# A decoder layer on one core: shared values tiles in cross attention, and self attention's buffers cleared earlier

## The reference

```
x = layernorm(x + self_attention(x))          # causal, scores relu(q k) * table(w, v), softmax, @ Wo + bo
x = layernorm(x + cross_attention(x, ctx))
x = layernorm(x + down(silu(gate(x)) * up(x)))   # int32 weights / 127, hidden size 1536

def cross_attention(query, ctx):
    q = query @ Wq.T + bq;  k = ctx @ Wk.T + bk;  v = ctx @ Wv.T + bv      # ctx: (32, 722, 512)
    probs = softmax(q k / sqrt(32))                                        # per head, over the 722 keys
    return (probs @ v) @ Wo.T + bo
```

## Time and profile before

| | |
|---|---|
| median of 3 runs | 2468.52 us (2468.2 to 2473.67) |
| the profiled execution | 2468.12 us |
| its span | 2466.3 us |
| PE busy | 2378.6 us (96%) |
| DVE, ACT, POOL busy | 1540.8 (62%), 1323.6 (54%), 1320.3 (54%) |
| chain that ended last | PE 74%, the D_ps_p units (L68) alone 42% |
| self attention | 0 to about 360 us |
| cross attention | 539 to about 1960 us |

### The profile page before, as it was taken

The page is one execution under the profiler, slowest core; times in us unless marked ns, Lnnn a source line. Parts: engine busy times, 40 slices in busy tenths (PEclk is TensorE's granted clock), DMA queues, the critical chain, the costliest instruction groups (busy, mean ns, idle before and its releaser), DMA issues.

```text
span 2466.3 us, 58741 instructions
## 1 busy us (share of the span) xinstructions
PE 2378.6 (96%) x21728; PEld 2050.7 (83%) x21728; DVE 1540.8 (62%) x2621; ACT 1323.6 (54%) x3287; POOL 1320.3 (54%) x1130
## 2 busy tenths in 40 slices
PE   7999968999999999999999999999999899999999
PEld 6887847888888888888888888888888698998998
DVE  7666677846666766666766667666676725335342
ACT  4777762116666666666666666666666651221311
POOL 4677563326565665656666566665655533333332
PEclk9999989999999999999999999999999999999999
DMA  6777676625767666666666676666767841101010
GB/s 196 198 224 203 191 201 251 242 104 147 191 187 195 188 183 187 189 191 190 185 189 187 190 192 186 185 188 188 196 187 191 233 149 64 39 26 61 2 39 23
DMA packets 271021, 404.21 MB, mean 164 GB/s; under 512 B 126364, under 2 KB 146332, under 8 KB 270748
## 3 DMA queue, kind: packets, MB, share of 16 engines
q1 hardware_dynamic: 246172, 350.25, 49.0%
q10 hardware_dynamic: 24576, 50.36, 8.1%
HBM read 134.11 MB, written 52.43 MB: 76 GB/s over the span
## 4 chain that ended last, share of the span: by engine, by line
PE 74%; DVE 1%; issue 1%; POOL 1%; ACT 0%; SPq 0%; DMA 0%; ACTq 0%; POOLq 0%; DVEq 0%
PE D_ps_p L68 42%; PE D_ps_s L1800 7%; PE D_ps_p L1826 6%; PE E_ps_g L68 5%; PE E_ps_u L68 5%; PE E_ps_d L68 5%; PE E_ps_y L68 3%; DVE D_columns L1611 0%; PE E_ps_t L1852 0%; SPq L1252 0%; DMA E_w_int<-in_w_gate 0%; ACT D_e L1476 0%; POOL D_e L1360 0%; DVE D_turned L1625 0%; POOL E_acts_low L1409 0%
## 5 line engine op out<-in xcount | busy, mean ns | idle before, releaser
L1360 POOL TENSOR_SCALAR D_e<-D_e,D_columns 128x722 f32<-128x722 f32 x256 | 538.9, 2105 | 528.2 <-DVE D_columns L1617 528.2
L1476 ACT ACTIVATE D_e<-D_ps_s,D_columns 128x723 f32<-128x723 f32 x512 | 438.2, 862 | 408.7 <-DVE D_columns L1611 358.2
L1611 DVE TENSOR_REDUCE D_columns<-D_ps_s 128x1 f32<-128x723 f32 x512 | 439.7, 900 | 303.1 <-PE D_ps_s L1800 302.9
L1625 DVE STREAM_TRANSPOSE D_turned<-D_e 128x768 f32<-128x768 f32 x512 | 496.4, 973 | 5.1 <-DMA D_pT<-D_turned 4.0
L68 PE MATMUL D_ps_p<-D_ctx_high,cross_wk_high 128*128 128x362 f32 (+1 forms) x1024 | 350.0, 342 | 1.5 <-DVEq L1637 1.5
L68 PE MATMUL D_ps_p<-D_ctx_low,cross_wk_high 128*128 128x362 f32 (+1 forms) x1024 | 336.6, 329 | 0.0
L68 PE MATMUL D_ps_p<-D_ctx_high,cross_wk_low 128*128 128x362 f32 (+1 forms) x1024 | 335.0, 327 | 0.0
L68 PE MATMUL D_ps_p<-cross_wv_high,D_ctx_high 128*128 128x512 f32 (+1 forms) x768 | 303.9, 396 | 0.0
L68 PE MATMUL D_ps_p<-cross_wv_high,D_ctx_low 128*128 128x512 f32 (+1 forms) x768 | 303.3, 395 | 0.0
L68 PE MATMUL D_ps_p<-cross_wv_low,D_ctx_high 128*128 128x512 f32 (+1 forms) x768 | 301.8, 393 | 0.0
L1483 ACT ACTIVATE D_e<-D_e,D_columns 128x722 f32<-128x722 f32 x256 | 230.9, 902 | 6.1 <-DVE D_columns L1617 6.1
(11 more groups left out here) (217 smaller groups left out, 5095.9 us busy)
## 6 DMA issues: line engine op xcount, KB each, us to landing
D_pT<-D_turned SPq DMA_DIRECT2D x1536, 96.0 KB, 2.7
D_pT<-D_turned ACTq DMA_DIRECT2D x512, 96.0 KB, 2.8
D_craw<-in_ctxT SPq DMA_DIRECT2D x124, 361.0 KB, 4.0
self_q<-A_q_out SPq DMA_DIRECT2D x10, 640.0 KB, 4.1
self_k<-A_k_out SPq DMA_DIRECT2D x10, 640.0 KB, 3.8
self_v<-A_v_out SPq DMA_DIRECT2D x25, 256.0 KB, 3.6
A_q<-self_q SPq DMA_DIRECT2D x32, 200.0 KB, 3.6
A_k<-self_k SPq DMA_DIRECT2D x32, 200.0 KB, 4.1
```

Of the source, the lines that this page charges most:

```text
L1360: pool.tensor_scalar(head, head, inv[:, 2 * (s % 2):2 * (s % 2) + 1], None, ALU.mult)\
L1476: act.activation(e[n // 2 % 2][:, n % 2, 0:PARTS * PART].rearrange("p (a c) -> p a c", a=PARTS), parts_of(n), ACT.Exp, bias=neg_max[:, n % ...
L1611: dve.tensor_reduce(neg_max[:, n % 4:n % 4 + 1], parts_of(n), AX.XY, ALU.max, negate=True)\
L1625: dve.transpose(turned[quad % 2][:, :, 2 * (s % 2) + h, :].rearrange("p j (t r) -> p t j r", r=32), e[s % 2][:, h, :].rearrange("p (t j r) ...
```

## The change

**Values.** Of the 32 batches the first 28 (`SHARED`) go in groups of four. The sixth values unit of a group's first three batches gets a stationary tile of its own, `tails`: columns 0 to 81 are the batch's own last 82 keys, columns 96 to 127 are a third (32, 32, 18) of the fourth batch's last 82 keys. ACT takes the first 82 rows as before, and the last rows, with a second copy, into `fourth`, one of two new tiles of 128 x 512. The fourth batch has no sixth unit, and its weighted sums read `fourth`. Batches 28 to 31 stay as they are.

The tails of a group are loaded by six DMAs of SP (`load_tails`), three with 82 and three with 32 or 18 columns, each of 128 x 4 runs; for the first group at the start behind the first queries, for the others in the third batch of the group before, behind `store`. POOL splits them (`split_tails`) in four pieces of 384 columns, in steps -6 to -3 for the first group, otherwise in steps 8b to 8b+3 of the last batch b of the group before. Two memsets of `fourth` stand among the six at the start, and `tails_raw` is cleared ahead of the wait for the queries.

**Self attention.** The clears of `e` and `pT[1]` move from behind the splits to the very beginning; the last split piece and the clear of `pT[0]` move behind the selection in the table.

```diff
                 pool.memset(minus_half[:, :], -0.5).then_inc(consts, 1)
+                for tile in e:
+                    pool.memset(tile[:, :, :], 0.0).then_inc(cleared, 1)
+                pool.memset(pT[1][:, :, :, :], 0.0).then_inc(cleared, 1)
...
-                for k in range(KD):
+                for k in range(KD - 1):
                     split_x(1, k)
-                for tile in e:
-                    pool.memset(tile[:, :, :], 0.0).then_inc(cleared, 1)
-                pool.memset(pT[1][:, :, :, :], 0.0).then_inc(cleared, 1)
-                pool.wait_ge(w_low, 3 * KD)
-                pool.memset(pT[0], 0.0).then_inc(cleared, 1)
                 pool.wait_ge(rhat_step, 2 * QUADS + 1)
...
+                split_x(1, KD - 1)
+                pool.memset(pT[0], 0.0).then_inc(cleared, 1)
...
+        for q in range(SHARED // 4):
+            for k in range(KD):
+                tail_at[PAIRS * (4 * q - 1) + k + (2 if q == 0 else 0)] = (q, k)
...
-            for i in range(ST):
+            for i in range(ST - is_fourth(b)):
                 unit_at.setdefault(PAIRS * (b - 1) + V_STEP[i], []).append(("v", b, i))
...
+                def load_tails(q):
+                    wait(sp, t_low, KD * q)
+                    for i in range(3):
+                        sp.dma_start(tails_raw[:, :, i * P:i * P + LAST], c_rows[4 * q + i, :, :, FULL:S])\
+                          .then_inc(t_loaded, 16)
+                    for i in range(3):
+                        first, end = FULL + THIRD * i, min(FULL + THIRD * (i + 1), S)
+                        sp.dma_start(tails_raw[:, :, (i + 1) * P - THIRD:(i + 1) * P - THIRD + end - first],
+                                     c_rows[4 * q + 3, :, :, first:end]).then_inc(t_loaded, 16)
...
+                    if b % 4 == 2 and b + 2 < SHARED:
+                        load_tails((b + 2) // 4)
                     move(QUADS * b + 1)
...
+                def split_tails(q, k):
+                    if k == 0:
+                        wait(pool, u_done, unit_count["v", 4 * q - 2, ST - 1] if q else 0)
+                        pool.wait_ge(t_loaded, 96 * (q + 1))
+                    pool.tensor_copy(tails[0][:, k, :], tails_raw[:, k, :]).then_inc(t_high, 1)
+                    pool.wait_ge(t_high, KD * q + k + 1)
+                    pool.tensor_tensor(tails[1][:, k, :], tails_raw[:, k, :], tails[0][:, k, :].bitcast(F32),
+                                       ALU.subtract).then_inc(t_low, 1)
...
                     act.activation(vs[b % 2][0:rows, i, :], bank("v", b, i)[0:rows, 0:D], ACT.Copy).then_inc(v_done, 1)
+                    if shares(b) and i == ST - 1:
+                        first = THIRD * (b % 4)
+                        size = min(THIRD, LAST - first)
+                        act.activation(fourth[b // 4 % 2][first:first + size, :],
+                                       bank("v", b, i)[P - THIRD:P - THIRD + size, 0:D], ACT.Copy).then_inc(v_done, 1)
...
                     for i in range(ST):
+                        values = fourth[b // 4 % 2] if is_fourth(b) and i == ST - 1 else vs[b % 2][:, i, :]
```

47 lines of the change are left out of this document (37 added, 10 removed).

## The result

The changed kernel took 2465.4 us (median of 12 runs, 2463.03 to 2470.92). The kernel before took 2473.35 us (12 runs, 2467.88 to 2479.41); the three shown above, median 2468.52, are among the twelve. The ratio is **0.9973, 95% interval 0.9964 to 0.9981**: 6.7 us faster (4.7 to 8.9), a little under the 0.3% that I had set as the bound for "faster". Forecast were 2459 us and, against the median it started from, a ratio of 0.9961. 2465.4 lies in the range of 2452 to 2467, near its end. Two things make up the distance: of the forecast gain of 9.6 us 6.7 came, and the median of the kernel before, from whose first three runs the forecast started, came out 4.8 us higher over twelve.

What follows compares the result with a forecast made beforehand. TensorE was taken as the bound in steady cross attention, with GpSimd close behind at its start and a table wait in self attention. Gains 9.5 + 7.9 less 7.8 make 9.6 us: 2468.5 to 2459, range 2452 to 2467.

Steps and rivals of the forecast that it cites:

- The seven units: Cross attention, each fourth batch: removing the sixth values unit gains 1.35 us, not its full 2.87; 9.5 us for seven.
- The other 21 batches: Cross attention's remaining sixth units, extra copies, tail splits and SyncE's six more DMAs, six times: cost put at nothing.
- VectorE waited for moves in batches 2, 6 and so on: Sign in cross attention: VectorE's transposition should not be released by a DMA in batches 2, 6, ... 22.
- The start of cross attention: Before batch 1's first keys unit: TensorE idles 5.7 us for GpSimd's pieces, the lower clock costs 2.1; 7.8 us lost.
- the forecast's 1.6 us ahead of the first subtraction: Start of cross attention: GpSimd's first subtraction comes 1.6 us later, at 557.8, behind tails landing at about 550.
- That the pause stayed at the first subtraction: Start of cross attention: GpSimd's 6.99 us pause is tied to its first subtraction, wherever that stands.
- Self attention: Moved clears and split piece: second scores 5.9 us earlier plus 2.0 us of clock; 7.9 us gained, at worst 3.
- From 60 us on DVE waits for PE, so both pass through: Self attention: the gains of 5.9 and 2.0 us are passed on past 60 us, sum 7.9 us.
- The 5.9 us at the second scores: Self attention: VectorE's table is undisturbed, so TensorE's second scores start at 46.4, not 52.30.
- The 2.0 us of clock: Self attention behind the second scores: the clock stays up through a 3.3 us pause, giving back 2.0 us; otherwise 0.
- Rival 2: Self attention to 100 us: ScalarE's chain and a falling clock leave 3 to 6 of 7.9 us; 2461 to 2464; chance 0.12.
- The early memsets: Start of self attention: GpSimd's clears beside VectorE's subtractions cost nothing; were they blocked, TensorE would start 1.4 us later.

Runs made afterwards that it cites:

- e6: Changed kernel with groups begun one batch later and the fourth batches' fifth values unit made in the sixth's step: 2445.68 us, ratio 0.9892 to the kernel before.
- e10: Changed kernel with the last six groups' six tail loads each issued twice, the second into an unread DRAM buffer: 2481.9 us, ratio 1.0035 to the kernel before.
- e9: Changed kernel with 20 extra matmuls in TensorE's 5.25 us pause before batch 1's first keys unit: 2463.37 us, ratio 0.9961 to the kernel before.
- e5: Changed kernel with groups begun one batch later and the two `fourth` clears moved behind GpSimd's reduction: 2457.32 us, ratio 0.9942 to the kernel before.
- e11: Changed kernel with groups one batch later, fourth batches' fifth values unit in the sixth's step, `fourth` clears behind the reduction: 2448.51 us, ratio 0.9903 to kernel before.
- e4: Changed kernel with 12 extra matmuls on TensorE in the pause behind self attention's second scores: 2465.13 us, ratio 0.9979 to the kernel before.
- e1: Kernel before with only the self attention part of the change, cross attention as it was: 2464.06 us, ratio 0.9975 to the kernel before.
- e8: Kernel before with only self attention's last split piece moved behind the selection, all clears where they were: 2472.61 us, ratio 1.000 to the kernel before.
- e7: Kernel before with only three of self attention's four clears moved to the beginning, all split pieces where they were: 2468.83 us, ratio 0.9986 to the kernel before.

## Why the prediction was right or wrong

- **The seven units: right.** Forecast 7 x 1.35 = 9.5 us; seven steps of 1.17 to 1.39 were read, 9.35 in all. The cause is shown by e6, in which TensorE's waits go away.
- **The other 21 batches: right in cost.** Between the steps the difference creeps by 0.05 to 0.1 us a group, 0.5 in all. Six SyncE issues took 3.6 us; VectorE waited for moves in batches 2, 6 and so on (1.20 us at 689.85, 11.9 us in all), which I had said it should not, and TensorE did not wait. e10 shows how near the edge that was.
- **The start of cross attention: right in size, in part by luck.** Forecast 5.7 + 2.1 = 7.8; from the first keys unit to the third scores it was 8.2. Second to third scores grew by 7.49: a stall of 5.25, the clock 2.1 (e9), the rest small. In the forecast's 1.6 us ahead of the first subtraction, 1.0 was a wait for the tails, and there was none: the last landed at 545.05, 3.0 us behind the queries and not 5.4, and GpSimd's cast began at 546.68. Yet the subtraction came 1.58 us later, counted from the first keys unit, since GpSimd's pause ahead of its reduction was 6.29 us where it had been 5.68, and the one behind the cast 7.52 where it had been 6.99. The first of these is longer in all nine kernels with tails (6.21 to 6.92, against 5.68 to 5.94 in the four without), and no run says why. That the pause stayed at the first subtraction was right: the subtraction came 8.08 us behind the cast, with 7.84 before, and with 1.06 us of memsets put behind the reduction it still came 7.82 (e5) and 7.93 (e11) behind it. The Trainium skill (GPSIMD Engine Reference, 2.1 Instruction dispatch) has a code load of about 6 us at the first call of a freshly loaded kernel; by its place and size the pause (7.52 us here) fits that, somewhat longer. Ahead of all this, the two clears of `fourth` delayed the first scores by 0.7 us. I had put them in front of GpSimd's pieces alone and overlooked that ACT, DVE and PE wait for the same count.
- **Self attention: the step that failed.** "From 60 us on DVE waits for PE, so both pass through. Sum 7.9 us". The 5.9 us at the second scores were 6.20. The 2.0 us of clock did not come, since the clock fell behind the pause of 3.32 us; and had it stayed, they would have been lost at the landing of the first moves (e4). So VectorE and TensorE do not simply wait for each other from 60 us on, as I had it: both wait for moved tiles. Of the 6.2, 5.4 were left at the fourth scores, 4.45 from 400 us on, and about 5.1 on the mean of ten executions at cross attention. The term was 7.9 and measured 5.1 by the profiles, 6.2 (3.5 to 8.7) by e1's times. Rival 2 had both kinds of loss, with 0.12, though it put the chain on ScalarE where e4 shows the landing of the moves.
- **The early memsets: right.** VectorE's four subtractions at the start took 1.70 us beside them, as in the earlier trace rows. They are operations with two inputs, and the memsets only write; the Trainium skill (SBUF — State Buffer, Who interferes with whom) sees no contention there, and this trace agrees.
- **A term that I did not have.** Where cross attention passes into the feed forward part, VectorE's transposition waits for moved tiles (5.47 us, before 3.96) beside the loads of the output weights, and that quad takes 10.99 us where it had 9.86. Over nine kernels with shared tiles it is 10.8 on average (9.87 to 11.72), over four without 9.95 (9.86 to 10.11): about 0.8 us. No run isolates its cause, so that stays open.

With these sizes the sum is 9.35 - 0.5 + 5.1 - 8.2 - 0.8 = 5.0 us, inside the 4.7 to 8.9 that were measured. What is also open is what makes cross attention start up to 5 us apart in kernels that are the same up to there, beyond the 1.5 us named above. In self attention TensorE waits for q and k to come back from DRAM and for moved tiles (28 us from 112 to 362 in the changed kernel) with the DMA engines at 69 to 77%, but nothing was varied there.

## What to carry to other kernels

Taking work out of the engine that is busy all the time gives its full price only where what it waits for next is ready. List what the other engines do ahead of that wait in their own order, and take the work out where that list is shortest: one index changed 7 x 1.35 us into 7 x 2.8. A buffer that is new to a steady loop has a first filling, and its place in the start-up, before anything is overlapped, can cost as much as the loop gains; beginning one turn later was free. In a stretch that waits for DMA round trips, count a gain in an engine's speed only as far as the next landing, and judge it over several executions.

## What the runs showed of the hardware

- Memsets of 2048 columns back to back on GpSimd held up single small VectorE operations on SBUF by several microseconds: 3.78 us for one that takes 0.36 (e8), 6.18 us for four that take 0.82. One of these four was held over four memsets, to within 0.1 us of the end of the last (40.39). A subtraction of GpSimd's held up one by 1.3 us (1.58 for 0.26, e7). Subtractions with two inputs beside memsets were not held up (1.70 us for four). VectorE's reciprocals of 400 columns took 2.65 us with or without memsets beside them.
- TensorE's clock was at its lower level behind idle pieces of 3.3 and 5.25 us (granted 0.50 from 50 to 54 and from 572 to 576 us), and stayed up (1.00) where 2.7 and 4.8 us of them were filled with matmuls whose results nobody reads (e4, e9).
- GpSimd's pause ahead of its first subtraction behind the reduction was 6.72 to 7.61 us in all 13 kernels, whether a tail or a piece of the context was subtracted. It moves with that subtraction: with two memsets (1.06 us) behind the reduction (e5, e11) the pause was 6.97 and 7.08 us, and the subtraction started 9.45 and 9.55 us behind the reduction's start, 8.37 to 9.15 in the six kernels that subtract a piece of the context there without these memsets.
